# An end stage of routed experts: 24 weight slots instead of 16, masks made just ahead of their use, rows prepared in half quarters

## The reference

```python
x = x + _L0_conv_ref(_ln_c(x), wq, bq, wk, bk, wv, bv, wo, bo, gamma, beta)
t = x.reshape(16, 128 * 128, 128)                       # rows (tokens) of 128
t = t + _L0_ffn_ref(_ln_t(t), gate_w, gate_b, weight1, weight2)

def _L0_ffn_ref(x, gate_w, gate_b, weight1, weight2):   # E = 64 experts, H = 512, K = 8
    probs = softmax(x @ gate_w.T + gate_b, axis=1)      # over the tokens of an image
    vals, idx = top_k(probs.transpose(0, 2, 1), K)      # 8 tokens for each image and expert
    pooled = einsum('bked,bke->bed', gathered, topv)    # weighted sum of the 8 normalised tokens
    h = gelu(einsum('ebd,edh->ebh', [pooled, 1], weight1))
    out = einsum('ebh,eho->ebo', [h, 1], weight2)
    weighted = out * topv                               # back to each of the 8 tokens
    return zeros.at[image, flat_idx].add(weighted)      # a token can be named by several experts
```

## Time and profile before

| | |
|---|---|
| median of three runs | 2205.4 us |
| the three runs | 2205.4, 2193.01, 2209.34 us |
| the profiled execution, its own time | 2199.44 us |
| span of its instructions | 2197.7 us |
| busy shares over the span | PE 88%, DVE 83%, ACT 85%, POOL 90% |
| main part, until the first gather | 1904 us |
| end stage | 294 us |
| mean granted clock of TensorE | 0.949 |

### The profile page before, as it was taken

How to read it: one execution, slowest core, us unless ns; L and a number is a source line. 1 busy time by engine, 2 the same in 40 slices (tenths; PEclk the granted TensorE clock), 3 DMA queues, 4 the chain that set the end, 5 groups by cost and what they waited for, 6 DMA issues and landing times.

```text
span 2197.7 us, 41739 instructions
## 1 busy us (share of the span) xinstructions
PE 1923.9 (88%) x11909; PEld 1289.9 (59%) x11909; DVE 1824.6 (83%) x4582; ACT 1866.6 (85%) x4791; POOL 1984.9 (90%) x2124
## 2 busy tenths in 40 slices
PE   6999999999999999999999999999999977456881
PEld 6866666666666666666666666666666633223561
DVE  4689899999999999999899999998999799513550
ACT  6999999999999999999999999999999988601220
POOL 5799999999999999999999999999999999461377
PEclk9999999999999999999999999999999999755895
DMA  5497888888888888888888888888887677813873
GB/s 192 153 263 206 227 222 225 224 222 208 228 218 225 213 222 218 228 226 221 225 228 212 216 226 219 226 212 224 217 229 206 159 189 188 237 47 108 231 180 32
DMA packets 111063, 447.88 MB, mean 204 GB/s; under 512 B 10575, under 2 KB 52404, under 8 KB 61684
## 3 DMA queue, kind: packets, MB, share of 16 engines
q1 hardware_dynamic: 81140, 302.61, 40.4%
q0 software_dynamic: 29696, 142.61, 36.2%
HBM read 306.78 MB, written 138.41 MB: 203 GB/s over the span
## 4 chain that ended last, share of the span: by engine, by line
POOL 45%; ACT 19%; issue 16%; PE 10%; DVE 4%; another core or an unknown queue 3%; DMA 2%; SPq 1%; POOLq 0%; ACTq 0%; DVEq 0%
POOL U L399 19%; POOL U L404 16%; ACT U L519 7%; POOL zn L420 5%; ACT zT L482 3%; POOL U L411 3%; ACT UT L476 3%; ACT LTS L491 2%; PE G L711 2%; POOL out_dram L454 1%; PE T L693 1%; ACT LTS L546 1%; PE O L644 1%; DMA U<-in_L_ffn_weight 1%
## 5 line engine op out<-in xcount | busy, mean ns | idle before, releaser
L519 ACT ACTIVATE U<-xa,nA,rA 128x128 f32<-128x128 f32 x1948 | 798.5, 481 | 0.6 <-issue 0.6
L711 PEld LDWEIGHTS G<-UT 128*128 128x128 f32 x4096 | 535.1, 192 | 231.2 <-issue 217.2
L399 POOL TENSOR_TENSOR U<-U,bet 128x512 f32<-128x512 f32 x512 | 652.5, 1274 | 3.5
L711 PE MATMUL G<-UT 128*128 128x128 f32 x4096 | 542.1, 275 | 0.4 <-DVE Gs L917 0.3
L404 POOL TENSOR_TENSOR U<-U,rO 128x512 f32<-128x512 f32 x512 | 532.8, 1041 | 3.5 <-ACT rO L500 3.5
L420 POOL TENSOR_TENSOR zn<-U,rZ 128x512 f32<-128x512 f32 x467 | 510.7, 1094 | 24.1 <-PE T L700 24.1
L644 PE MATMUL O<-U,MT 128*128 128x512 f32 x1024 | 527.7, 597 | 0.0
L912 DVE BATCH_NORM_STATS2 stA<-xa 128x6 f32<-128x256 f32 x1024 | 385.1, 423 | 70.9 <-POOL nA L386 42.2
L894 DVE BATCH_NORM_STATS2 stO<-O 128x6 f32<-128x256 f32 x1024 | 385.0, 419 | 35.9 <-PE O L644 34.4
L700 PE MATMUL T<-ident,zn 128*128 128x128 f32 x2048 | 326.9, 283 | 76.2 <-POOL zn L420 53.5
L990 DVE BATCH_NORM_STATS2 stZ<-U 128x6 f32<-128x256 f32 x1024 | 385.3, 420 | 9.7 <-DMA U<-in_x 9.6
(11 more groups left out here) (148 smaller groups left out, 1652.3 us busy)
## 6 DMA issues: line engine op xcount, KB each, us to landing
xa<-in_x SPq DMA_DIRECT2D x128, 1024.0 KB, 5.8
U<-in_x POOLq DMA_DIRECT2D x128, 1024.0 KB, 8.1
out_dram<-U SPq DMA_DIRECT2D x128, 1024.0 KB, 7.1
U<-in_L_ffn_weight SPq DMA_DIRECT2D x128, 256.0 KB
xa<-out_dram,UT POOLq DMA_INDIRECT x64
out_dram<-U,UT POOLq DMA_INDIRECT x64
U<-in_L_ffn_weight SPq DMA_DIRECT2D x1, 128.0 KB
LTS<-in_L_conv_wq SPq DMA_DIRECT2D x1, 64.0 KB
```

Source lines behind the costliest of these rows:

```text
L399: gp.tensor_tensor(rows(a, i), rows(a, i), bet_b, ALU.add).then_inc(S["gb"], 1)
L519: last = sc.activation(utile(a, i, j), xa[:, k % XR, h * W:(h + 1) * W], ACT.Identity, scale=rA[:, k % 2, h:h + 1], bias=nA[:, k % 2, h:h ...
L711: last = te.matmul(G[:, 0:P], v, v, start=(i == 0 and j == 0), stop=(i == NI - 1 and j == TI - 1))
```

## The change

What it does, in five parts:

1. **Weight ring.** 24 slots (`WR`), 6 groups. The 8 new ones lie in the other half of `U` (4 experts, loaded when the last image is stored) and in `LTS` (4 experts, loaded when the last exponentials are done). Expert e waits for layer 2 of group (e - 24) // 4.
2. **Masks.** `codes(u)` and `equal(u)` move from slot u to slot u+6, one slot ahead of `combine(u)`. `EQ` keeps two units instead of eight; this is the room for the four experts. `codes(u)` and `equal(u)` stay at their place inside a slot.
3. **Prepare.** `prepare` and `scales` work on 8 images at a time. Half 0 of the next quarter is done in the slots with t mod 4 = 1, half 1 in those with t mod 4 = 2. Quarter 0 has both halves ahead of slot 0.
4. **Pooling** waits for each half on its own.
5. `OUTs`, `first`, `b1s` and `b2s` move to `zT`; SyncE loads the biases behind the four experts 16 to 19.

```diff
+WR = 24
-        wring = U[:, 0, :, :].rearrange("p k n -> p (k n)").rearrange("p (e n) -> p e n", e=EQN)
+        wparts = [U[:, 0, :, :].rearrange("p k n -> p (k n)").rearrange("p (e n) -> p e n", e=EQN),
+                  over(half, 4, 2 * HID, at=at_h),
+                  LTS[:, :, :].rearrange("p a n -> p (a n)").rearrange("p (e n) -> p e n", e=4)]
...
-        EQ = over(half, 2, NB, P, at=at_h)
+        EQ = over(half, 2, 4, P, at=at_h)
...
-                if e >= EQN:
+                if e >= WR:
-                    sp.wait_ge(R_["o"], (e - EQN) // 4 + 1)
+                    sp.wait_ge(R_["o"], (e - WR) // 4 + 1)
...
+            for e in range(EQN, EQN + 4):
+                weights(e)
+            sp.wait_ge(S["lg"], NB * NI // 2)
             sp.dma_start(b1s, w1[:, W, :]).then_inc(s_bias, 16)
             sp.dma_start(b2s, w2[:, HID, :]).then_inc(s_bias, 16)
-            for e in range(EQN, E):
+            sp.wait_ge(S["seg_exp"], NB * NS)
+            sp.wait_ge(S["seg_i"], NB * NS)
+            for e in range(EQN + 4, E):
                 weights(e)
...
-            def scales(q):
+            def scales(q, h):
...
-                if t < NG and t % 4 == 2 and t // 4 + 1 < Q:
-                    scales(t // 4 + 1)
+                if t < NG and t % 4 in (1, 2) and t // 4 + 1 < Q:
+                    scales(t // 4 + 1, t % 4 - 1)
...
             def pooling(q):
-                pe.wait_ge(R_["fw"], q + 1)
                 wait(pe, R_["p_done"], q)
-                for n in range(NB):
-                    last = te.matmul(T0[:, n * EQN:(n + 1) * EQN], R[:, q, n, :], FW[:, q % 2, n, :], start=True, stop=True)
-                last.then_inc(R_["pmm"], 1)
+                for h in range(2):
+                    pe.wait_ge(R_["fw"], 2 * q + h + 1)
+                    for n in range(8 * h, 8 * h + 8):
+                        last = te.matmul(T0[:, n * EQN:(n + 1) * EQN], R[:, q, n, :], FW[:, q % 2, n, :], start=True, stop=True)
+                    last.then_inc(R_["pmm"], 1)
...
-                pe.wait_ge(s_w[g % 4], 128 * (q + 1))
+                pe.wait_ge(s_w[g % (WR // 4)], 128 * (g // (WR // 4) + 1))
...
-                if t < NG:
-                    codes(t)
+                if 0 <= t - 6 < NG:
+                    codes(t - 6)
...
-                wait(dve, R_["cmm"], u - 7)
+                wait(dve, R_["cmm"], u - 1)
...
-                if t < NG:
-                    equal(t)
-                if t < NG and t % 4 == 2 and t // 4 + 1 < Q:
-                    prepare(t // 4 + 1)
+                if 0 <= t - 6 < NG:
+                    equal(t - 6)
+                if t < NG and t % 4 in (1, 2) and t // 4 + 1 < Q:
+                    prepare(t // 4 + 1, t % 4 - 1)
```

More of the change, by code:

```diff
@@ L150, in program @@
         HTs = over(half, 2, HID, at=at_h)
-        OUTs = over(half, 2, W, at=at_h)
+        OUTs = over(spare, 2, W, at=at_t)
         OT = over(half, 2, NB, P, at=at_h)
-        first = over(half, 4, P, at=at_h)
-        b1s = over(half, HID, at=at_h, parts=E)
-        b2s = over(half, W, at=at_h, parts=E)
+        first = over(spare, 4, P, at=at_t)
+        b1s = over(spare, HID, at=at_t, parts=E)
+        b2s = over(spare, W, at=at_t, parts=E)
         FW = over(half, 2, NB, EQN, at=at_h)
@@ L194, in program @@
         s_sc = [sem(f"s_sc{i}") for i in range(4)]
-        s_w = [sem(f"s_w{i}") for i in range(4)]
+        s_w = [sem(f"s_w{i}") for i in range(WR // 4)]
         tnames = ("sel part cut code rowf idx codt codc row eq fst nf idxs rbn rvar rln rr wv cen fw pmm p_done "
@@ L572, in _ @@
             bodies(act, body)
-            def scales(q):
[L575 to L579, removed]
+            def scales(q, h):
+                p, x = q % 2, 2 * q + h
+                f = slice(8 * h, 8 * h + 8)
+                act.wait_ge(R_["rvar"], x + 1)
+                sc.activation(sR[:, p, f], vR[:, p, f], ACT.Ln).then_inc(R_["rln"], 1)
+                act.wait_ge(R_["rln"], x + 1)
+                wait(act, R_["wv"], x - 3)
+                sc.activation(rR[:, p, f], sR[:, p, f], ACT.Exp, scale=-0.5).then_inc(R_["rr"], 1)
             def pooled(q):
-                act.wait_ge(R_["pmm"], q + 1)
+                act.wait_ge(R_["pmm"], 2 * q + 2)
                 wait(act, R_["h"], 4 * (q - 1))
@@ L1025, in _, with prepare @@
             ve.tensor_copy(CT, G[0:E, 0:P]).then_inc(R_["codc"], 1)
[L1027 to L1035, removed]
+            def prepare(q, h):
+                p, x = q % 2, 2 * q + h
+                f = slice(8 * h, 8 * h + 8)
+                dve.wait_ge(s_rows[q][h], 128)
+                for m in range(4):
+                    n = 8 * h + 2 * m
+                    last = ve.bn_stats(stR[:, p, n:n + 2, :].rearrange("p n s -> p (n s)"),
+                                       R[:, q, n:n + 2, :].rearrange("p h w -> p w h"))
@@ L1036, in prepare @@
                 last.then_inc(R_["rbn"], 1)
[L1037 to L1040, removed]
+                dve.wait_ge(R_["rbn"], x + 1)
+                wait(dve, R_["rln"], x - 3)
+                ve.tensor_scalar(vR[:, p, f], stR[:, p, f, 2], 1.0 / W, EPS_T, ALU.mult, ALU.add).then_inc(R_["rvar"], 1)
@@ L1041, in prepare @@
+                ve.tensor_tensor(R[:, q, f, :], R[:, q, f, :], stR[:, p, f, 1].unsqueeze(2).to_broadcast([P, 8, W]),
                                  ALU.subtract).then_inc(R_["cen"], 1)
[L1042 to L1048, removed]
+                dve.wait_ge(R_["rr"], x + 1)
@@ L1050, in equal @@
+                ve.tensor_tensor(wvb[:, p, f], TQ[:, q, f, 0], rR[:, p, f], ALU.mult).then_inc(R_["wv"], 1)
+                dve.wait_ge(R_["wv"], x + 1)
+                dve.wait_ge(R_["cen"], x + 1)
+                wait(dve, R_["pmm"], x - 3)
+                ve.tensor_tensor(FW[:, p, f, :], fold[:, :].unsqueeze(1).to_broadcast([P, 8, EQN]),
+                                 wvb[:, p, f].unsqueeze(2).to_broadcast([P, 8, EQN]), ALU.mult).then_inc(R_["fw"], 1)
             def equal(u):
@@ L1061, in equal @@
                 wait(dve, R_["nf"], 2 * u - 1)
-                ve.tensor_tensor(first, EQ[:, q % 2, f, :], before.unsqueeze(1).to_broadcast([P, 4, P]), ALU.mult).then_inc(R_["fst"], 1)
+                ve.tensor_tensor(first, EQ[:, u % 2, :, :], before.unsqueeze(1).to_broadcast([P, 4, P]), ALU.mult).then_inc(R_["fst"], 1)
                 dve.wait_ge(R_["fst"], u + 1)
@@ L1072, in _ @@
                 dve.wait_ge(s_store[NK + n], 16 * (NB // 2))
-            prepare(0)
+            for h in range(2):
+                prepare(0, h)
             for t in range(SLOTS):
```

28 lines of the change are left out of this document (17 added, 11 removed).

## The result

The changed kernel takes 2184.7 us (median of 9 runs, 2182.0 to 2188.8) against 2205.4 (9 runs, 2193.0 to 2209.4): a ratio of 0.991, interval 0.9895 to 0.9926, 20.7 us less. The forecast was 2185. The profiled executions stand at 2182.0 and 2199.4, 17.4 us apart, where 15.0 was forecast.

The account below looks back on a forecast made before the run. The first scatter, then GpSimd's scatters, were taken to bound the end; gains of 6.5 + 2.0 + 0 + 3.7 + 2.8 = 15.0 us off 2199.4 gave 2184.4, say 2185, range 2148 to 2200.

Parts of the forecast that it names:

- Bound and sum: End stage: the end moves one for one with the first scatter; five terms sum to 15.0 us gained.
- the 2041 to 2045 given: Sign that the forecast is right: GpSimd's first scatter starts at 2041 to 2045 us, against 2056.2 before.
- the stall: TensorE, VectorE and ScalarE held up from about 1949 to 1998, beside the gathers; forecast to stay as before, 60%.
- (a): Slots 2 to 5 lose four mask products on TensorE: 6.5 us gained; slots 6 and 7 keep one each.
- (b): Preparing in halves removes TensorE's wait for the copy `OT` in slot 3: 2.0 us gained.
- the 3 estimated: Quarter 0 pooled in halves starts before its last row lands: 3 us, lost again if the stall keeps its end.
- (c): Nine more table loads on ScalarE, 11.5 us in all, taken to cost 0 beside TensorE's work.
- (d): TensorE's waits for weights in slots 6 and 7, ahead of the first scatter, go: 3.7 us gained.
- (e): GpSimd's first gap between scatters shrinks if the clock stays up without slot 7's weight wait: 2.8 us gained.
- cost 0: Loading eight experts early, at 1907 to 1925 beside only the gathers, was taken to cost nothing.
- the signs given: `HTs` of group 0 at 1992 or later, second gelu not before 1970, pooling of quarter 1 at about 2004.
- The case without a stall: Rival: the change removes or shortens the hold-up from 1949 on; 47 to 57 us less, about 2150 us; 20%.

Follow-up runs that it names:

- a20m: The changed kernel with 20 weight slots and the masks back in their old place: 2147.1 us, 10.5 more than with 20 slots and late masks.
- aprep: The changed kernel with quarters prepared, scaled and pooled whole as before: 2143.4 us, on a chip without the stall.
- again: The changed kernel without any edit, on another chip, without the stall: 2134.4 us, ratio 0.988 to the kernel before.
- p1: The changed kernel with pauses in the gathers of quarters 2 and 3: 2134.9 us without the stall; run again on a chip with it, 2170.1, ratio 0.986.
- f1: The changed kernel with images 0 to 14 of quarters 0 and 1 gathered first, then image 15 of both: 2189.0 us, ratio 0.992.
- x_half: The changed kernel with quarters 2 and 3 loaded by plain transfers from fixed places, timing only: 2148.5 us, ratio 0.974.
- late: The changed kernel with experts 16 to 23 loaded only once image 15's indices are there: 2183.9 us, ratio 0.990.

## Why the forecast came true, step by step

**Bound and sum.** Right: the time follows the first scatter (15.9 us earlier, 17.4 us less time in the profiled executions). It came at 2040.3, just outside the 2041 to 2045 given. But that the sum came so close is in part luck. Ahead of the first scatter it had 12.2 us (masks, halves, weights), and behind it 2.8; the traces have 15.9 and 1.5. The 15.9 are, from the two timelines of TensorE: 7.4 of masks, 3.7 of weights, 1.3 lost on waits for `OT`, and 5.5 because the same passes ran at the upper clock, 2.6 of them in the pooling of quarter 1 (granted clock 0.81 from 1999.5 to the first scatter, 0.67 before from 1997 on). The remaining 0.7 is how far TensorE had come when the stall ended. The clock's part was in my range, but not in the sum, and it covers what the halves did not give.

**(a) Masks, 6.5.** Right in kind and low. In slots 2 to 7 the kernel before has six products, 9.7 us, the kernel after two of 1.16: 7.4. The sum counted slots 2 to 5 and called 6 and 7 even, but slot 7's product ran at 2.07 before:

```profile
2048.07 2.07 PE L780 MATMUL G<-zn,ident 64*128 64x128 f32 x8
```

Without the stall it is 10.5 in all (a20m).

**(b) Halves, 2.0.** The step that failed. The wait for `OT` left slot 3 and came back in others: before, TensorE waited 1.98 us in slot 3; now it waits 0.44, 0.90 and 1.94 at 2022.5, 2028.6 and 2036.2 (slots 5 to 7), 1.3 us worse. The one of 0.44 isn't the halves': aprep has it too. Without the stall the one in slot 3 doesn't go at all (3.30 in again, 3.08 in aprep); there the halves gain 1.2 us from `HTs` of group 0 to the first scatter (48.3 in again, 49.5 in aprep), and p1 takes 49.5 as well, so a gain in the slots is not shown. What the halves give is the early start, 1.2 to 3.7 us there against the 3 estimated; with the stall it is lost, as the forecast said.

**(c) Table loads, 0.** Right: aprep has nine fewer and gains nothing in its slots. In p1_again:

```profile
1957.55 1.28 ACT L602 ACT_TABLE_LOAD   x1
1958.85 0.21 ACT L602 ACTIVATE UT<-UT 128x8 f32<-128x8 f32 x1
```

The load of 1.28 us at 1957.55 is followed by the next ACTIVATE at 1958.85, no drain of 1380 ns between, so the rule of the Trainium skill ("ScalarE: Activation LUTs", "What ACT_TABLE_LOAD costs") again doesn't hold in these rows.

**(d) and (e) Weights and clock, 3.7 + 2.8.** Right: no wait for weights, the first gap 6.2 instead of 8.6 (2.4), the gaps 13.6 instead of 16.5 in sum. The pooling of quarter 1 takes 3.98 us at the upper clock, 6.56 before, a gain that I had not placed there:

```profile
2008.09 3.98 PE L751 MATMUL T<-U,xa 128*128 128x16 f32 x32
```

All scatters from the first to the last gained 1.5 us, not the 2.9 of the gaps. Alone, 16 slots instead of 20 cost 9.0, with a wait of 5.5 us ahead of the first scatter where the kernel before had 3.7. That the waits grow once the masks are gone would fit; the kernel before has no trace without the stall to compare. Also wrong, and small: the early experts "cost 0". They fill the queues from 1907 to 1925, and VectorE's wait was longer with them: 4.2 to 5.9 us in four traces (p1_again, f1, after, x_half), 3.7 and 3.8 in the two without them (late, before). That would be where the last gather's 1.9 us come from.

**The stall.** "As before" was right for its end: 6.8 us behind the last gather's end, 7.2 before. Three of the signs given were wrong: `HTs` of group 0 came at 1973.5, not 1992 or later; the second gelu at 1962, not after 1970; the pooling of quarter 1 at 2008.1, not 2004, as `layer2(0)` was caught in the stall and the last gather came later. My statement that nothing was late before 1949 was wrong too: VectorE's 3.76 us ahead of the sum, from 1918 on, was the same thing. The case without a stall, which I had as a rival, is real, but by its times the kernel before has it as well, in the same groups; so the change does not bring it about. I put it 35 us below the forecast; it is 50.

## What to carry to other kernels

When engines stand idle beside a long row of indirect DMAs and nothing in the program makes them wait, try the same kernel on a second chip, or at another time, before pricing an edit there: here that moved the time by 46 to 50 us, the change by 21 to 25. Put such gathers where they can be spread, with a pause every few us, or into idle time ahead of the stage; more gathers in place of a pause can cost as much as they save. And price the parts of a change with the cover taken away too: a part that is hidden on one chip counts on the other. Last, add up the terms after the run as well: a sum can come true while one of its terms did not.

## What the runs showed of the hardware

In the groups with before at 2205.4, 2204.8 and 2198.2, gathers that GpSimd issues every 1.25 us hold up TensorE, VectorE and ScalarE. It takes a while of gathers without a pause until it begins. In the kernels before and after it was 14 us from the first gather on and about 20 us from the next pause on; in x_half, late and the second row of p1_again, where plain transfers ran beside the gathers, 11 to 15 us. What sets this length is not shown. VectorE is held up even between two of its own instructions (5.21 us, f1). The gathers themselves keep their pace, at 52 GB/s: the packets of one are over about 2 us behind the start of its issue, in the stall (1958.5 in the kernel after) as outside it (1928.65 in the kernel before). The DMA engines are busy for 0.20 of the time in the stall and for 0.70 and more beside the same gathers without it, so it is not their traffic. Two groups show nothing of it, by their seven traces, and going by the times in all their 56 runs.

What holds the engines up is open. The Trainium skill, "NOTIFIC — the notification-queue block", section "Interfaces", says that the block that writes the records of a profile holds its producers back when an internal FIFO fills, and that this can stall an engine. Instructions in the stall that leave one by one (passes 2.8 us apart in the earlier trace rows, 0.7 at 1998.04 and 1998.74 in the kernel after) would fit that, but no run here was made without recording, so it is not shown, nor whether an unrecorded execution stalls at all.
